# A graph layer kernel on one core: four split buffers instead of three, and splits three slots ahead

## What is computed

```
h   = relu(layernorm(x))                       # x: 4096 x 256
d   = rowsum(adj) ** -0.5, 0 where rowsum <= 0 # adj: 4096 x 4096, f32
out = x + relu((d[:, None] * adj * d[None, :]) @ h @ W + b)
```

## Time and profile before

| | us |
|---|---|
| median of three executions | 403.66 |
| the profiled execution, its own time | 404.6 |
| its span, first to last instruction | 402.7 |
| TensorE busy | 388.9 |
| VectorE busy | 313.7 |
| ScalarE busy | 283.6 |
| GpSimd busy | 113.2 |

### The profile page before, as it was taken

One profiled execution on the slowest core, in us unless ns is written; L12 is line 12 of the kernel. 1 busy time (PEld: TensorE's weight loads), 2 busy tenths in 40 slices (PEclk: granted clock), 3 DMA queues, 4 the chain that ended last, 5 costly groups with the idle time before them and its releaser, 6 DMA issues.

```text
span 402.7 us, 5083 instructions
## 1 busy us (share of the span) xinstructions
PE 388.9 (97%) x1728; PEld 322.6 (80%) x1728; DVE 313.7 (78%) x316; ACT 283.6 (70%) x279; POOL 113.2 (28%) x273
## 2 busy tenths in 40 slices
PE   3999989999999999999999999999999999999995
PEld 2888868888888888888888888888888888878884
DVE  4877686868788896958688687859748697899996
ACT  2699776887777778777769658877777868345532
POOL 2350522525533335312224522422113223000000
PEclk9999989999999999999999999999999999999999
DMA  8999999999999999899999999999969998789566
GB/s 272 426 417 358 426 418 425 418 424 418 422 422 419 422 378 376 335 404 410 371 367 331 418 409 348 409 422 422 347 263 426 425 419 311 293 343 356 148 188 243
DMA packets 23048, 149.50 MB, mean 371 GB/s; under 512 B 2800, under 2 KB 3056, under 8 KB 6384
## 3 DMA queue, kind: packets, MB, share of 16 engines
q1 hardware_dynamic: 23024, 149.19, 93.1%
HBM read 144.97 MB, written 4.21 MB: 370 GB/s over the span
## 4 chain that ended last, share of the span: by engine, by line
PE 96%; ACT 1%; DVE 1%; DMA 1%; issue 1%; SPq 0%; ACTq 0%; DVEq 0%
PE moved L726 22%; PE moved L728 22%; PE moved L727 22%; PE held L728 7%; PE held L726 7%; PE held L727 7%; PE held L696 4%; PE moved L696 3%; PE moved L679 2%; DMA at<-in_x 1%; ACT turned L382 1%; DVE acc L586 0%; ACT hi L375 0%; DVE stats L527 0%; ACT acc L398 0%
## 5 line engine op out<-in xcount | busy, mean ns | idle before, releaser
L375 ACT ACTIVATE hi<-at,s 128x1024 fp32r<-128x1024 f32 x112 | 123.2, 1144 | 65.4 <-issue 48.0
L726 PE MATMUL moved<-hi,G 128*128 128x512 f32 x384 | 150.3, 392 | 1.9 <-DVE acc L586 1.9
L589 DVE TENSOR_TENSOR acc<-moved,acc 128x1024 f32<-128x1024 f32 x84 | 102.8, 1224 | 62.2 <-PE moved L728 62.0
L727 PE MATMUL moved<-lo,G 128*128 128x512 f32 x384 | 150.0, 391 | 0.0
L728 PE MATMUL moved<-hi,G 128*128 128x512 f32 x384 | 150.0, 390 | 0.0
L570 DVE SCALAR_TENSOR_TENSOR lo<-at,s,hi 128x1024 fp32r<-128x1024 f32 x112 | 140.8, 1277 | 3.6 <-ACT hi L375 3.6
L362 ACT ACTIVATE nat<-nat 128x2048 f32<-128x2048 f32 x64 | 121.6, 1903 | 9.8 <-DMA nat<-in_adj 9.8
L726 PEld LDWEIGHTS moved<-hi,G 128*128 128x128 f32 x384 | 72.4, 188 | 17.7 <-DVE acc L586 2.3
L728 PEld LDWEIGHTS moved<-hi,G 128*128 128x128 f32 x384 | 72.5, 189 | 15.2
L727 PEld LDWEIGHTS moved<-lo,G 128*128 128x128 f32 x384 | 72.5, 189 | 15.0
L488 POOL TENSOR_TENSOR row_sum<-part 128x1 f32<-128x1 f32 x32 | 21.3, 667 | 185.6 <-ACT nat L362 185.3
(11 more groups left out here) (54 smaller groups left out, 217.3 us busy)
## 6 DMA issues: line engine op xcount, KB each, us to landing
nat<-in_adj SPq DMA_DIRECT2D x64, 1024.0 KB, 8.6
at<-in_adj_t SPq DMA_DIRECT2D x64, 1024.0 KB, 8.7
nat<-d_dram SPq DMA_DIRECT2D x2, 1024.0 KB, 5.9
nat<-in_x_t SPq DMA_DIRECT2D x4, 512.0 KB, 4.0
turned<-in_x_t SPq DMA_DIRECT2D x4, 512.0 KB, 5.6
out<-nat SPq DMA_DIRECT2D x4, 512.0 KB, 4.9
at<-in_x SPq DMA_DIRECT2D x3, 512.0 KB, 7.1
turned<-in_x SPq DMA_DIRECT2D x3, 512.0 KB, 12.6
```

What stands on the lines that cost most here:

```text
L375: nc.scalar.activation(hi[g % RING][:, 2 * c:2 * c + 2, :], at[g % LA][:, 2 * c:2 * c + 2, :], ACT.Copy, scale=s[:, j:j + 1]).then_inc(hi_ ...
L589: nc.vector.tensor_tensor(out=own, in0=pair[:, :, :], in1=own, op=ALU.add).then_inc(taken, 1)
L726: nc.tensor.matmul(into[:, f, :], big, hi[g % RING][:, t, :], start=begins, stop=False)
L727: nc.tensor.matmul(into[:, f, :], big, lo[g % RING][:, t, :], start=False, stop=False)
```

## The change

Four hi and four lo buffers instead of three. A new function, `split_in(g)`, gives the slots that are split in the turn of slot g: up to slot 3 slot g + 2 as before, in slot 4 both slot 6 and slot 7, from slot 5 on slot g + 3. ScalarE's and VectorE's loops use it, VectorE with its tiles dealt over the two gathers. The nat table has one more block from slot 5 on (11 and 12 in slot 5, 13 in slot 6, and so on). The scratch area for dynamic DMA is set to 1024 bytes.

```diff
--- before.py
+++ after.py
@@ -69,7 +69,7 @@
 
     table, m = [], 2 * WIDTHS[0]
     for g in range(len(SLOTS)):
-        end = min(2 * WIDTHS[0] + min(2 * (g + 1), g + 3) + max(0, g - 17) // 7, 2 * NB)
+        end = min(2 * WIDTHS[0] + min(2 * (g + 1), g + 3) + (g > BASE[1]) + max(0, g - 17) // 7, 2 * NB)
         table.append(range(m, end))
         m = end
     return table
@@ -81,6 +81,14 @@
 def summed_in(j):
 
     return next((g for g in range(len(SLOTS)) if 2 * j + 1 in NATS[g]), 0)
+
+
+def split_in(g):
+
+
+    if g < BASE[1]:
+        return [g + 2]
+    return [s for s in ([g + 2, g + 3] if g == BASE[1] else [g + 3]) if s < len(SLOTS)]
 
 
 def scale_slots():
@@ -119,7 +127,7 @@
     HALF = N // 2
     LN = 3
     LA = 4
-    RING = 3
+    RING = 4
     ROT = 2
     LX = 4
 
@@ -415,13 +423,14 @@
             for g, (k, q, _) in enumerate(SLOTS):
 
 
-                ahead = g + 2 < len(SLOTS) and SLOTS[g + 2][1] != 0
-                if ahead:
-                    round_slot(g + 2)
+                for slot in split_in(g):
+                    if SLOTS[slot][1] != 0:
+                        round_slot(slot)
                 for m in NATS[g]:
                     sum_nat(m)
-                if not ahead and g + 2 < len(SLOTS):
-                    round_slot(g + 2)
+                for slot in split_in(g):
+                    if SLOTS[slot][1] == 0:
+                        round_slot(slot)
                 if q == 0 and k in TURNING:
                     take_turned(TURNING[k])
                 if q == 0 and k in PROJECTING:
@@ -637,16 +646,13 @@
                     subtract(g, c)
                 rest_of_raw(3 + g)
             for g, (k, q, panels) in enumerate(SLOTS):
-                if NARROW[k] and NARROW[SLOTS[g + 2][0]]:
-                    for p in range(2):
+                tiles = [(slot, c) for slot in split_in(g) for c in range(2 if NARROW[SLOTS[slot][0]] else 1)]
+                for p in range(2):
+                    if NARROW[k]:
                         gather(k, 2 * q + p)
-                        subtract(g + 2, p)
-                elif NARROW[k]:
-                    for p in range(2):
-                        gather(k, 2 * q + p)
-                    subtract(g + 2)
-                elif g + 2 < len(SLOTS):
-                    subtract(g + 2)
+                    half = len(tiles) // 2
+                    for slot, c in (tiles[half:] if p else tiles[:half]):
+                        subtract(slot, c)
                 if q == 0 and k in PROJECTING and PROJECTING[k] < RAW:
                     rest_of_raw(PROJECTING[k])
                 if q == 0 and k in MEASURING:
@@ -776,7 +782,7 @@
         "in_w": np.ascontiguousarray(w),
         "in_b": np.ascontiguousarray(b.reshape(dim // P, P).T),
     }
-    nc = bacc.Bacc("TRN2", target_bir_lowering=False, num_devices=1)
+    nc = bacc.Bacc("TRN2", target_bir_lowering=False, num_devices=1, dynamic_dma_scratch_size=1024)
     args = [nc.dram_tensor(name, a.shape, mybir.dt.from_np(a.dtype), kind="ExternalInput").ap()
             for name, a in arrays.items()]
     d_dram = nc.dram_tensor("d_dram", (P, NB), F32).ap()
```

## The result

The change made the kernel slower: 410.55 us median (409.61 to 411.34, six runs) against 403.36 (402.28 to 407.16, six runs) before, ratio 1.0166, 95% interval 1.0127 to 1.0206. The interval is clear of no difference. The forecast was 407.6 us with a range up to 409.6: the direction of its likeliest case holds, its size doesn't, and the time lies outside the range. A kernel slower by over 1% had been given 0.36, one that can't be told from the kernel before 0.56.

A forecast was written before the change was run, and what follows sets the result against it. TensorE was taken as the bound, its matmuls following without a hole from 58 to 350 us. Profiled 404.6 + 2.2 (stall) + 1.7 (clock) = 408.5, less 0.9 to the median: 407.6 us, range 403.2 to 409.6.

The forecast's parts named there:

- likeliest case: New TensorE stall in slot 6's second panel, 2.2 us plus 1.7 for the clock: 407.6 us, chance 0.45.
- The old hole: TensorE's stall near 51 us, waiting for a VectorE gather in the product loop; forecast to stay, 0 change.
- The new one: Slot 6, second panel: TensorE waits for a gather behind slot 8's low part, restarting at 73.8; loss 2.2 us.
- Slot 9: Its first high tile is done at 76.0, the gather behind it due at 78.2, so no second stall.
- after 80 us no hole: Sign that the forecast is right: TensorE's row shows no idle gap after 80 us.
- The term for the clock: Lower TensorE clock after the new stall in slot 6 adds 1.7 us, bounds 0 and 1.7.
- In steady state the load, split and release of a buffer keep their distances: Between start and end only their distance to TensorE grows, by a slot; TensorE's 292.0 us without a hole give cover.
- The end: Slot 60's split in slot 57: gather done at 371.1 against a deadline of about 370.8; taken as 0, up to 2.
- The row sum: At the end the last row sum is done 1.9 us earlier, and with it the loads ahead of slot 60's.
- The 0.9 us taken off: Whole kernel: the profiled 404.6 us stood 0.9 over the median of 403.66, so 408.5 became 407.6.
- The slower one: Rival, chance 0.12: stall paid twice, again in slot 7's second panel through slot 9, or at the end; 409.8 us.
- the case of no effect: Rival, chance 0.15: ScalarE waits for loads wherever the lead was to be won, so time is unchanged; 403.5 us.

The follow-up runs named there:

- splits alone: The change with the old nat table: 412.28 us, ratio 1.0227; with slot 27's load also issued ahead of slot 24's nat loads: 407.49 us, ratio 1.0096.
- two ahead at the end: The change, with splits only two slots ahead again from slot 57 on: 408.59 us, ratio 1.0125 to the kernel before.
- three repairs: The change with sums and splits reordered in slots 4 and 5, slot 8's and 27's loads ahead of nat loads, two-ahead splits from slot 57: 406.77 us.

## Why the prediction was wrong

**What held.** The old hole stayed (2.1 us of idle time after, 1.9 before). The new one is where it was forecast and, but for the clock, of its size: in the second panel of slot 6, for a gather behind the low part of slot 8, ScalarE standing 4.13 us (4.4 in the text) for slot 7's block. Forecast were a loss of 2.2 us and a restart at 73.8; the trace has 2.2 us (the starts 2.28 us apart, less a matmul of 0.227, and a slow second one) and 74.46, with all 0.6 us later from the start. Slot 9 held without a second stall, as worked out. Of the signs given, "after 80 us no hole" failed.

**The term for the clock, 1.7, was 0 in the profiled run**, and yet something like it is in the medians. Idle times of TensorE of 1.8 to 1.9 us went either way in these runs (last section). The Trainium skill (TensorE: Matmul & The Clock Gate, "Why this matters for your kernels") warns only of gaps over about 3 us; the falls after 1.8 to 2 us contradict it, and this one hole alone would bear it out. The two traces have one fall each, so their difference of 5.8 us holds none; the medians are 7.2 apart. The granted clock of each execution, which is known without a trace too, points to the rest. In the 14 profiled executions it was 0.997 to 1.0 where TensorE fell to the lower clock at none of the holes (4), 0.992 to 0.995 with one fall (6) and 0.988 to 0.990 with two (4). Of 63 executions of the kernel before, 40 have 0.997 or more, with a median of 403.2 us, and 22 have 0.992 to 0.996, with a median of 405.1. All six of the change have 0.995 or less, two of them 0.989 or less. So the median execution of the kernel before most likely had no fall, its profiled one had one (404.6, 1.2 over the median), and the change nearly always pays at least one. That is read from mean clocks; no trace shows where in those executions the clock fell.

**"In steady state the load, split and release of a buffer keep their distances": this step failed.** It compared at blocks with at blocks. But in the turn of slot 22 the place of the sum against the split changed with the lead, because the slot that begins a step is now split one turn earlier. The sum came 6.6 us later, 3.6 more than the delay so far, and by way of the nat load and SyncE's queue the at load of slot 27. I had gone through the queues at slots 4 to 9 and not at slot 24, where the table takes two nat blocks again and where there is a projection too. Worth 1.0 us in the profile of the change, and 4.9 us where slot 6 is mended (the runs on splits alone).

**The end was taken at 0: this step failed too, and cost 1.8 us by the traces** (2.0 by the medians of the run with two ahead at the end). The forecast asked whether the gather comes before slot 59 needs it, and it does: it began at 373.14 and slot 59 at 374.58. It didn't ask what 3.27 us of standing VectorE mean in a stage where VectorE has the most to do: 5.88 us from the start of slot 60's low part (369.79) to that of the next slot's (375.67), against TensorE's 5.44 for a slot. It can't catch up, so slots 60 and 61 and the last adds come late. The row sum that was to save this is a sum earlier, but the load of slot 60 left at 358.83, which is 354.82 and the 4.0 us by which everything was later: it waits for the last G, not for the row sums.

**The sum, put right.** The 0.9 us taken off stood for the distance of the profiled execution from the median; the term of 1.7 for the clock behind the new hole did not come in the profile, but the medians differ by about one fall. So these two came out right by luck. The forecast of 407.6 lacks 1.0 for slot 25 and 1.8 for the end; with them it is 410.4, against 410.55.

**The rivals.** The slower one had the right sign and nearly the size (409.8), and half of the place: slot 9 was not the second payment in the change, but the end, which it named with up to 2 us, was. Slot 9 is one in the run of three repairs, 1.71 us in slot 7, from slot 9's block at 74.67 where 74.8 had been worked out. As for the case of no effect, no placing of the lead was free, but from slot 28 on it costs little.

## What to carry to other kernels

Where an engine's order interleaves preparing work with collecting work that the bound engine needs, moving the preparation earlier helps only if its data are there earlier; ask for each such pair when the data land, not how far ahead the result is. When a lead changes, walk every queue at the irregular places (first step, a slot with an additional load, a projection, the last stage), and not only through one steady turn. And put work that nobody waits for (a sum for a later step) behind the work that somebody does: that alone gained 0.7% here (ratio 0.9934), and it took the whole loss away where the nat table had caused it.

## What was not expected of the hardware

- The granted clock of TensorE went to the lower level for 3.4 us after single idle times of 1.82, 1.87, 1.88, 1.91, 1.94 us and more (up to 3.83), and not after 1.43, 1.49, 1.65, 1.68, 1.71, 1.74 nor, once, 1.89 us. In the profile of the kernel before one such stretch cost 1.7 us. So a kernel with one hole of this length most likely has executions of two kinds; by their mean clocks those of the kernel before have medians of 403.2 and 405.1 us.
- With the line of loads full, 1 MB lands every 2.5 us in order of issue, and a load may be 16.5 us under way. The time of issue hardly matters then: slot 10's block was issued at 62.99 before and at 66.54 with the splits alone, and landed at 77.31 and 76.94. What stands ahead of it in the queue does: in the change, with the additional nat block ahead of it, it landed at 80.38, of which 1.0 is a later start.
- The first product matmul came at 31.3 to 33.0 us in the profiled runs, whose program is the same up to there, as the clock at the start rose at 11.9 to 14.8 us: over 1 us of difference between executions that the edits don't explain.
